# A two-layer convolution kernel on one core: gram products, output copies, a copy of x and the sums of slopes placed elsewhere in a unit

## What is computed

```python
# layer 0
aTa = jnp.einsum('bpi,bpj->bij', vec_a, vec_a)
attn = jax.nn.softmax(aTa, axis=-1)
aaTa = jnp.einsum('bpc,bcj->bpj', vec_a, attn)
return gamma * aaTa + x
# layer 1
x = (x - xmin) / (xmax - xmin + EPS)
measures = jnp.stack([_box_sum(x, k) for k in SCALES], axis=-1)   # SCALES = 2, 4, 8, 16
log_m = jnp.log(measures + EPS)
alphas = jnp.einsum('bhwcs,s->bhwc', log_m, lr_c) / jnp.sum(lr_c ** 2)
squeeze = alphas.mean(axis=(1, 2))
excite = jax.nn.sigmoid(jax.nn.relu(squeeze @ w1 + b1) @ w2 + b2)
...
sim = (a * b).sum(-1) / (jnp.linalg.norm(a, axis=-1) * jnp.linalg.norm(b, axis=-1) + EPS)
alpha_norm = (alphas - moving_mean) / jnp.sqrt(moving_var + BN_EPS) * gamma + beta
x = x * excite[:, None, None, :]
return sim * jax.nn.sigmoid(alpha_norm) + (1.0 - sim) * x
```

## Time and profile before

| | |
|---|---|
| median of 3 runs | 6241.43 us (6239.41 to 6245.17) |
| the profiled execution | 6245.49 us, its span 6243.6 us |
| VectorE busy | 5222.7 us, 84% of the span |
| TensorE busy | 4976.2 us, 80% |
| ScalarE busy | 4828.5 us, 77% |
| GpSimd busy | 1806.9 us, 29% |
| TensorE clock granted, mean | 0.915 of full speed |
| moved by DMA | 1344.68 MB, 215 GB/s over the span |

### The profile page before, as it was taken

How to read it: one execution, slowest core, us unless ns; L and a number is a source line. 1 busy time by engine, 2 the same in 40 slices (tenths; PEclk the granted TensorE clock), 3 DMA queues, 4 the chain that set the end, 5 groups by cost and what they waited for, 6 DMA issues and landing times.

```text
span 6243.6 us, 108779 instructions
## 1 busy us (share of the span) xinstructions
PE 4976.2 (80%) x35320; PEld 4609.1 (74%) x35320; DVE 5222.7 (84%) x6293; ACT 4828.5 (77%) x5203; POOL 1806.9 (29%) x1361
## 2 busy tenths in 40 slices
PE   6968888699969998699969998799968887666632
PEld 5758888688858888688858887688857777566621
DVE  1348999799979999799979999799989999788820
ACT  0117888599959999599959999599959998688843
POOL 0012332233332333233323333333323332333311
PEclk9989999899989999899979999899979998788855
DMA  3544655588968988588858888589857777566678
GB/s 122 179 157 149 191 189 176 160 267 267 268 175 239 270 268 248 165 269 268 268 161 247 268 269 249 162 267 269 269 158 230 230 237 226 146 183 188 181 182 202
DMA packets 874514, 1344.68 MB, mean 215 GB/s; under 512 B 38704, under 2 KB 694096, under 8 KB 857936
## 3 DMA queue, kind: packets, MB, share of 16 engines
q1 hardware_dynamic: 800592, 1073.93, 49.1%
q0 software_dynamic: 73728, 268.47, 23.7%
HBM read 671.16 MB, written 536.87 MB: 193 GB/s over the span
## 4 chain that ended last, share of the span: by engine, by line
PE 36%; ACT 27%; issue 17%; DVE 10%; DMA 9%; ACTq 1%; POOL 1%; DVEq 0%; SPq 0%; POOLq 0%
PE even L545 14%; PE h_ps L526 8%; ACT logs L725 4%; ACT logs L763 4%; PE g_ps L503 4%; ACT logs L750 3%; ACT odd L725 3%; ACT logs L753 3%; DMA ut<-logs 3%; PE odd L554 3%; ACT logs L749 2%; DMA qd<-p_scratch 2%; PE o_ps L563 2%; ACT xt L712 2%; DMA hr<-h_scratch 2%
## 5 line engine op out<-in xcount | busy, mean ns | idle before, releaser
L545 PE MATMUL even<-band,t 128*128 128x128 f32 x12288 | 1871.0, 284 | 277.3 <-ACT logs L725 275.9
L545 PEld LDWEIGHTS even<-band,t 128*128 128x128 f32 x12288 | 1638.2, 199 | 330.5 <-issue 330.5
L407 POOL TENSOR_TENSOR t<-t 128x1024 f32<-128x1024 f32 (+3 forms) x800 | 1353.2, 1704 | 1034.1 <-DVE logs L1045 902.8
L526 PE MATMUL h_ps<-mix,xt 128*128 128x256 f32 x4096 | 994.1, 385 | 192.4 <-ACT xt L712 190.0
L526 PEld LDWEIGHTS h_ps<-mix,xt 128*128 128x128 f32 x4096 | 737.5, 190 | 322.4 <-ACT xt L712 242.0
L432 POOL DMA_DIRECT2D ut<-logs x256 | 224.6, 877 | 2588.4 <-DVE logs L1061 2508.4
L725 ACT ACTIVATE logs<-even,col 128x1024 f32<-128x1024 f32 x512 | 570.6, 1114 | 403.7 <-PE even L545 393.8
L547 PE MATMUL even<-band,t 128*128 128x128 f32 x4096 | 792.2, 275 | 0.0
L503 PE MATMUL g_ps<-xa 128*128 128x257 f32 x2048 | 621.9, 385 | 23.7 <-DMA xa<-in_x_dram 23.7
L563 PE MATMUL o_ps<-ident,qd 128*128 128x128 f32 x2048 | 359.2, 304 | 349.1 <-ACT o_sb L790 205.1
L930 DVE CUSTOM_DVE_ANT_0 h_out<-h_ps,shift,mx 128x512 f32<-128x512 f32 x512 | 383.0, 748 | 293.5 <-PE h_ps L526 289.6
(11 more groups left out here) (185 smaller groups left out, 10100.0 us busy)
## 6 DMA issues: line engine op xcount, KB each, us to landing
xa<-in_x_dram SPq DMA_DIRECT2D x256, 512.0 KB, 8.6
xb<-in_x_dram SPq DMA_DIRECT2D x256, 512.0 KB, 8.5
h_scratch<-h_out SPq DMA_DIRECT2D x128, 1024.0 KB, 8.7
hr<-h_scratch SPq DMA_DIRECT2D x256, 512.0 KB, 6.8
q_scratch<-logs SPq DMA_DIRECT2D x256, 512.0 KB, 4.6
ut<-logs POOLq DMA_DIRECT2D x256, 512.0 KB, 6.5
p_scratch<-ut SPq DMA_DIRECT2D x256, 512.0 KB, 2.6
qd<-q_scratch SPq DMA_DIRECT2D x256, 512.0 KB, 8.3
```

The costliest lines, as they stand in the source:

```text
L407: ins = g.tensor_tensor(dst[:, hf, d:d + n, :], src[:, hf, d:d + n, :], src[:, hf, e:e + n, :], ALU.add)
L526: ins = t.matmul(h_ps[:, r * C:(r + 1) * C], xt[:, q % 2, jh, r, :], mix[:, jh, :], start=(jh == 0), stop=(jh == 1))
L545: ins = t.matmul(o, src[:, hf, at, :], band[:, which, :], start=True, stop=(which < 3))
```

## The change

TensorE's first half of a gram step moves from ahead of the first box to behind the turn of x that follows it, ahead of the third box. On ScalarE the copy of x moves ahead of the last step of the sigmoid. The second output half (d = 1) of a unit is copied one unit later, behind the offset and ahead of the log of the third box; one more such copy stands at the end of a turn. On VectorE L1023 writes its sums into 32 columns, one for each chunk and half of an image, at an address held in a register; `add_slopes` reduces all of them once, in the stretch after the turn, where it also replaces the clearing of `ACC`. Counts of a semaphore follow.

```diff
-DVE_MIN_PAIR, DVE_PAIR, DVE_IMAGE = 4, 32, 381
+DVE_MIN_PAIR, DVE_PAIR, DVE_IMAGE = 4, 30, 365
-        slope = sb("slope", [128, 4])
+        slope = sb("slope", [128, 2 * CHUNKS])
+        def two_behind(i, k, hf):
+            at = 2 * k + hf
+            return (i, at - 2) if at > 1 else (i - 1, at + 2)
 # TensorE, half_chunk
-                if A:
-                    gram_rows(n, hf, 0)
                 if Cs:
                     box(u, k, hf, 0, first)
                 if Bs:
                     turn_x(nb, 2 * hf)
+                if A:
+                    gram_rows(n, hf, 0)
                 if Cs:
                     box(u, k, hf, 2, first)
 # ScalarE, half_chunk (second: the second unit of a turn)
                     offset(u - 1, nC if hf == 1 else nC - 1, 1 - hf)
+                if Ds and not first and not second:
+                    copy_out(ud - 2, *two_behind(8 * (s - 3) + i, k, hf), 1)
                 if Cs:
                     log(u, hf, 2)
...
                 if tail:
-                    sigmoid(u - 1, 1 - hf, (1, 2))
+                    sigmoid(u - 1, 1 - hf, (1,))
                 if Bs:
                     copy_xt(nb, 2 * hf + 1)
                 if tail:
+                    sigmoid(u - 1, 1 - hf, (2,))
                     invert(u - 1, 1 - hf, (0,))
                 if Ds and not first:
                     copy_out(ud - 1, *behind(8 * (s - 3) + i, k, hf), 0)
                 if tail:
                     invert(u - 1, 1 - hf, (1, 2, 3))
-                if Ds and not first:
-                    copy_out(ud - 1, *behind(8 * (s - 3) + i, k, hf), 1)
 # ScalarE, turn, after the loop
                 if Ds:
+                    copy_out(32 * (s - 2) - 2, 8 * (s - 2) - 1, 2, 1)
                     for d in range(2):
                         copy_out(32 * (s - 2) - 1, 8 * (s - 2) - 1, 3, d)
 # VectorE
-            def linear(unit, k, hf, cubed):
-                at = 2 * hf + k
+            def linear(unit, i, k, hf, cubed):
+                at = CHUNKS * hf + 2 * i + k
+                to = slope[:, at:at + 1] if isinstance(at, int) else slope[:, bass.ds(at, 1)]
-                                       accum_out=slope[:, at:at + 1]).then_inc(slopes, 1)
+                                       accum_out=to).then_inc(slopes, 1)
-            def add_slopes(unit, k):
+            def add_slopes(unit):
                 dve.wait_ge(slopes, unit + 1)
-                by_half = slope[:, :].rearrange("p (h k) -> p h k", k=2)
-                d.tensor_tensor(cols(ACC), cols(ACC), by_half[:, :, k], ALU.add).then_inc(dve_done, own.one())
+                d.tensor_reduce(cols(ACC), slope[:, :].rearrange("p (h n) -> p h n", h=2), AX_X, ALU.add).then_inc(dve_done, own.one())
                 dve.wait_ge(dve_done, own.now())
-                if Cs and hf == 0 and tail:
-                    add_slopes(v, 1 - k)
-                if Cs:
-                    d.memset(cols(ACC), 0.0).then_inc(dve_done, own.one())
```

More of the change, by code:

```diff
@@ L791, in copy_out, with half_chunk @@
                              o_ps[:, :].rearrange("p (r c) -> p r c", c=CH), ACT.Copy).then_inc(o_copied, 1)
-            def half_chunk(s, i, k, hf, A, Bs, Cs, Ds, first):
+            def half_chunk(s, i, k, hf, A, Bs, Cs, Ds, first, second):
                 n = 16 * s + 2 * i + k
@@ L836, in pair @@
                         for hf in range(2):
-                            half_chunk(s, i, k, hf, A, Bs, Cs, Ds, first and k == 0 and hf == 0)
+                            half_chunk(s, i, k, hf, A, Bs, Cs, Ds, first and k == 0 and hf == 0, first and k == 0 and hf == 1)
                 pair(0, True)
@@ L1101, in half_chunk @@
                 if Cs:
-                    linear(u, k, hf, cubed)
+                    linear(u, i, k, hf, cubed)
                 if A and ending:
@@ L1150, in turn @@
                     two = two_squares(u - 1, 1)
-                    add_slopes(u - 1, 1)
+                    add_slopes(u - 1)
                     three = three_squares(u - 1, 1, two)
```

## The result

| | before | after |
|---|---|---|
| median of 5 runs | 6241.43 us (6239.41 to 6245.38) | 6310.47 us (6303.27 to 6316.87) |
| ratio | | 1.0108, 95% interval 1.0094 to 1.0122 |
| span of the profiled execution | 6243.6 us | 6315.0 us |
| VectorE, ScalarE busy | 5222.7, 4828.5 us | 5208.7, 4802.8 us |
| DMA rate over the span | 215 GB/s | 213 GB/s |

The changed kernel is slower by 1.1%, 69 us, where 78 us less were forecast. Of the outcomes named beforehand rival B, about 6315 us, is the nearest.

What follows compares the result with a forecast made beforehand. Bound: VectorE's chain through GpSimd (L1045, row sums, stalled L1007), ScalarE close behind and the bound in turn 8. Savings 3 + 26 + 18 + 6 + 27 - 2 = 78 us from 6241.4 give 6163, own range 6135 to 6195.

Steps and rivals of the forecast that it cites:

- rival B: SyncE's queue: 3 us delay reaches ut's landing undiminished, L1007 waits 1.9 in 80 units, 152 us; about 6315; chance 0.08.
- The chain that sets a unit: Turn 5: L1045, 4.9 to 5.2 us of GpSimd, L1007 stalled until GpSimd finishes, VectorE to next L1045; about 19.4 after.
- The slopes: VectorE: half of the units lose the addition L1029, 0.08 us per unit in all 256; nothing taken for register addressing.
- Turn 8: 32 units bound by ScalarE, whose round gets shorter: 0.55 us per unit, 18 us saved, between 5 and 24.
- Turn 2: Only the slopes count there: 32 units at 0.08, 3 us saved.
- Turn 9: No copy of x, only the output copy: 0.2 us per unit, 6 us saved, between 0 and 15.
- what is queued behind the late copy: SyncE's chunk store and loads go some 3 us later in alternate units; 0.3 us delay likely, costing 0.02 per unit.
- the room of 1.2 us: Accumulating DMA into ut lands 8.9 us after L1061, L1007 wants it 10.1 after; the likely 0.3 delay fits.
- The Trainium skill's rule of the round over the queues: DMA engines serve queues packet by packet, so GpSimd's transfer would not stand behind SyncE's backlog; delay term then 0.
- Turn 10: Output stage: scaling right behind the first copy, 1.8 us less per pair, 27 us; 10 to 38 if q's load limits.
- The gram: TensorE's half gram moved past the first box: first log earlier, nothing shortened on VectorE by itself, nothing in turns 8 to 10.
- the shares of ScalarE's round: Late output copy 0.5 and moved copy of x 0.15 shorten ScalarE's round to some 18.9 us, below VectorE's.

Runs made afterwards that it cites:

- e3_store_after: The changed kernel with SyncE issuing the store of an output chunk behind the loads instead of ahead of them; 6143.7 us, 0.9843 of before.
- e9_pool_half: Changed kernel, store behind loads, gram moved only where C runs, GpSimd's t8 row sums over 64 of 128 columns (result not computed); 6049.9 us, 0.9688 of before.
- e12_late_and_store: The kernel before with only the late second output copy and the store behind the loads; 6191.9 us, 0.9916 of before.
- e10_x_copy_back: Changed kernel, store behind loads, gram moved only where C runs, copy of x back behind the sigmoid's last step; 6157.5 us, 0.9862 of before.
- e8_slopes_back: Changed kernel, store behind loads, gram moved only where C runs, slopes added in every second unit as before; 6149.5 us, 0.9848 of before.
- e5_gram_only: The kernel before with the half gram moved in all turns and nothing else; 6239.8 us, 0.9994 of before.
- e4_hold: The kernel before, but SyncE waits ahead of a chunk's store until ScalarE's offset of that unit is done; 6319.8 us, 1.0128 of before.
- e7_gram_back: The changed kernel with the store behind the loads and the half gram in its old place in all turns; 6141.7 us, 0.9834 of before.
- e2_copy_late: The kernel before with the late second output copy alone; 6334.0 us, 1.0145 of before.

## Why the prediction was wrong, point by point

**The chain that sets a unit: right.** A settled unit was expected near 19.4 with all waits off the chain; with the queue freed (e3_store_after) it is 19.31 to 19.33 in the mean of 20 units, in every turn from 3 to 7. That L1007 stands for GpSimd is shown by e9_pool_half.

**The slopes: right,** 0.08 per unit (19.31 and 19.39), and nothing to be seen of the register's cost. **Turn 8: right in kind, small in size:** 24.4 for 18, just over its bound of 24. By the experiments 14 of it go with the late copy (e12_late_and_store) and 11 with the copy of x (e10_x_copy_back). **Turn 2:** 3.8 for 3, a near hit that is in part luck. The slopes alone were counted; they are worth 2.2 there (e8_slopes_back), while the copy of x earns 5.6 beside them (e10_x_copy_back) and the gram moved by itself costs 4.6 (e5_gram_only). **Turn 9:** 2.5 for 6, within its bounds.

**The step that failed is "what is queued behind the late copy".** It had the right places (SyncE's queue, the addition into ut, the room of 1.2 us) and the right hold (some 3 us, measured 3.1), and gave 0.3 us of delay and 0.02 per unit. The landing moved by 2.0 us in the units shown, from 8.9 to 10.9 after L1061's like, and by 1.5 in the median of the units with a store. In place of 3 us lost over 160 units, turns 3 to 7 lost 94 (3152.3 - 3058.2), and against what they reach with the queue freed, 136. Two things had been left out. The first is a second one who waits: the store of p is issued when ut has landed, and the offset on ScalarE waits for p's store; I had followed the landing to VectorE alone. The offset's 164.7 us of waiting are twice L1014's 83.3. The second is the order: the copy now stands behind the offset, so that the delay can feed itself, and ScalarE, made faster by the same change, comes to that wait earlier. Of these two I have no measure; e4_hold, where ScalarE is no faster, loses 77 of the 94.

Rival B had the mechanism with 152 us; its 6315 is 5 us off, and that is luck in part. It let the landing come 3.2 us later, which is twice what was measured, named L1007's wait alone, and kept a gain of 27 us for turn 10 that did not come.

By the table the changed kernel is 94.1 us longer in turns 3 to 7, 12.3 up to the start of C and 0.9 in turn 10, and shorter by 3.8, 24.4 and 2.5 in turns 2, 8 and 9: 76.6 more. The stretches between turns give back 5.2 to the 71.4 by which the spans differ.

The Trainium skill's rule of the round over the queues ("DMA: Bandwidth & Descriptors", "Queues, rings and completion order"), by which the delay would have been 0, does not help here: a transfer of 0.5 MB on GpSimd's queue landed 2 us later when the same 2.5 MB on SyncE's queue were issued 1 to 3 us later. My reading is that taking turns does not keep the two from sharing what the DMA engines can move, so that the delay goes with how much the other queue still has to move. No run tests that apart.

**Turn 10: wrong.** 27 us were expected and none came (226.6 for 225.7). The scaling did move ahead, but the round changed over to the load of q, as the bound of the text said it might, and at once. ScalarE and SyncE in turn 10 of the kernel after:

```profile
6186.09 1.24 ACT L744 ACTIVATE qd<-qd,col 128x1024 f32<-128x1024 f32 x1 [6.07 <-DMA qd<-q_scratch]
...
6189.51 1.23 ACT L744 ACTIVATE qd<-qd,col 128x1024 f32<-128x1024 f32 x1
...
6190.82 0.60 ACT L795 ACTIVATE o_sb<-o_ps 128x512 f32<-128x512 f32 x1
...
6191.66 0.41 SPq L306 DMA_DIRECT2D out_dram<-o_sb  x1
6192.44 1.61 SPq L282 DMA_DIRECT2D qd<-q_scratch  x2
```

The scaling of 6186.09 had waited 6.07 us for its load; the loads go out at 6192.44, behind the store of the copy of 6190.82, which stands behind the second scaling. Late copy and load are one round there. It takes 15.2 us from this scaling to its like at 6201.29, and 14.6 for a pair in the mean of the turn, as before. With the loads ahead of the store (e3_store_after) the turn takes 189 us in place of 227: the gain is there (37 us) once the queue lets it.

**The gram: wrong on both sides.** It was taken at nothing. In turn 1 it costs 12 us, a stage in which I had not looked for it: the text asked only what it does where C runs. In turns 3 to 7 it earns 23 us by itself. It and the copy of x both shorten TensorE's way from the mix of x to the first box, and with the store out of the way either of them is enough for the 19.31 of turn 5; after the one, the other earns 1 us (e7_gram_back) or 7 (e10_x_copy_back) in turns 3 to 7. The late copy shortens ScalarE's way between the same two points, and alone it is worth nothing there (e12_late_and_store); that TensorE's way is then as long is my reading of it. I had added the shares of ScalarE's round up as if ScalarE alone made it.

Whether the offset's wait or VectorE's weighs more was not tried apart, but the traces allow an estimate. Take the 150 inner units of turns 3 to 7, in the changed kernel against e3_store_after. From the product ahead of GpSimd's row sums to the minimum behind L1014 they take 8.09 us each in place of 7.55, 81 us in all. VectorE's own waits for the addition make an estimated 51 of these: added up, L1014 ends 56 us later than GpSimd (its end plus 1.05 us) and VectorE would let it, and 5 in e3_store_after. From the minimum to the next product, where ScalarE's late L758 counts, the units take 12.64 in place of 12.27, 56 us. So of 137 us about 51 are VectorE's own waits, and 86 come by way of ScalarE and TensorE, which wait for the store of p. In e2_copy_late, against the kernel before, it is the other way about: of 112 us in such units VectorE's own waits make an estimated 89.

## What to carry to other kernels

Before an instruction is put later, list the DMAs that wait for it and everything behind them in the queue that issues them; then follow each landing to all who wait for it, through stores that are themselves issued on a landing. A store that waits for computing belongs behind the loads that wait for nothing, and here that exchange of two steps turned 1.1% slower into 1.6% faster; without the late copy it was worth nothing (1.0004). Read a moved instruction in each stage of the program, also in those where its neighbours are missing.

## What the runs showed that I had not expected

How soon a DMA landed depended on how close ahead of it the others were, at the same volume. In the units shown, the addition into ut took 2 us more when the 2.5 MB of stores and loads were issued within 2.9 us just ahead of it than when they were issued over 5.0 us and earlier (10.9 and 8.9 us after L1061's like). It is the loads that count: in e3_store_after the store of the chunk is issued just as late (4.0 us ahead of L1069 in the median of turns 3 to 7, 3.3 in the changed kernel), but the load of q 7.3 us ahead in place of 0.3, and the addition lands after 8.6 us in place of 10.7.

And a mean over units can hide two kinds of them. With GpSimd's work cut the 12 units of turn 5 still take 19.32 in the mean, as if another engine set them; ten of them take 18.67 to 19.09, as in turn 2, and two units carry the rest.
